# Looking up 4-bit weights: maxima of four neighbouring lines in one VectorE reduction

## The chip, the cores and the metric

The kernel runs on one core of one Trainium2 chip. The metric is the device time of one execution in microseconds (us), the median of the runs given. Lower is better.

## The reference

A decoder layer: self-attention, cross-attention, and a gated feed-forward stage whose three weight matrices are stored as 4-bit codes with one scale for each 64 codes. The change concerns the last stage alone:

```
NF4_CODE = [-1.0, -0.696, -0.525, -0.395, -0.284, -0.185, -0.091, 0.0,
            0.080, 0.161, 0.246, 0.338, 0.441, 0.563, 0.723, 1.0]
def dequant_nf4(q, absmax, shape):
    w = NF4_CODE[q.reshape(-1)]
    w = w.reshape(-1, 64) * absmax[:, None]
    return w.reshape(shape)
g = einsum('bsh,mh->bsm', x, Wg);  u = einsum('bsh,mh->bsm', x, Wu)
h = silu(g) * u
return einsum('bsm,hm->bsh', h, Wd)      # B*S = 2048, H = 1024, M = 3584
x = x + ffn(layernorm(x), ...)
```

## The kernel before

The program has two parts, one after the other: `attention` (up to about 930 us of the profiled execution) and `feed_forward`. Every engine runs its own list of instructions in the order of the code; semaphores are the only ties between them.

**The feed-forward stage.** The 3584 hidden features are worked in 14 groups of two chunks of 128. For each group the TensorE multiplies the normalised input with the gate and up weights (`gate_up`, L1507: 8 steps `q`, each one chunk against 512 columns, 24 matmuls for gate and 24 for up) and then adds the group's share of the output (`down`, L1527: 16 row blocks `r`, 12 matmuls each). Every product is three fp16 matmuls (high by high, high by low, low by high). Group 0 is written out, because the layer norm and the transposes of the input run within its first steps; groups 1 to 12 are a hardware loop; group 13 is written out again.

**A weight tile** is 128x512 codes. There are 12 a group, and they are worked six tiles ahead of their use. A tile goes through these steps:

1. SyncE loads codes and scales (`load`).
2. ScalarE draws eight lines (`draw_line`, L1553 and L1556): an affine function of the code each, an fp32 plane of 128x512. The code table, taken as a function of the code, is the maximum of four upper lines less the maximum of four lower lines. The first of each four is clamped at zero (`Relu`), the others are `Copy` with scale and bias.
3. VectorE takes three maxima on each side, pair by pair (L1631), and the difference of the two (L1637) into `w32`: seven operations, `LUT = 7` (`look_up`).
4. GpSimd multiplies by the scales (L1432), ScalarE casts to fp16 (`cut_high`, L1561), GpSimd computes the rest that fp16 lost (`cut_low`, L1437).

There is one set of eight planes, `line`. ScalarE draws one tile ahead of VectorE, so line `m` of the next tile may be drawn once VectorE has read line `m` of this one: that is the wait on `lut` in `draw_line`.

**The order around it.** `CUTS` (and `FIRST_CUTS` in group 0) says how many look-up operations VectorE has done by each step `q`. In groups 1 to 12 ten tiles lie in the eight gate and up steps and two in `down`, one operation behind each `add_down` (L1672). Each step's list on VectorE ends with `hidden(q)` (L1667), which needs the `silu` of that step from ScalarE (`gate_silu`, L1584) and the up product. ScalarE's lists follow the same cuts one tile later: `silu` stands three quarters through the lines of its step, `hidden_high` (L1589) behind the second line, `cut_high` behind the third line of a tile. TensorE has two banks each for gate, up and down: gate step `q` needs `silu(q - 2)`, down block `r` needs `add_down(r - 2)`, and `add_down(0)` stands behind `hidden(7)` on VectorE.

Of the kernel before, what the change touches and what calls it, by code (L numbers as in the profile page):

```python
# [8 lines left out]
FP32 = mybir.dt.float32  # L9
# [3 lines left out]
ALU = mybir.AluOpType  # L13
ACT = mybir.ActivationFunctionType
AX_X = mybir.AxisListType.X
# [6 lines left out]
P = 128  # L22
# [8 lines left out]
HALF = 512  # L31
# [17 lines left out]
def code_line(lo, hi):  # L49

    slope = np.float32(F_SCALE * (NF4[hi] - NF4[lo]) / (hi - lo))
    return float(slope), float(np.float32(F_SCALE * NF4[lo] - float(slope) * lo))
# [4 lines left out]
UPPER_LINES = [code_line(8, 9), code_line(10, 11), code_line(12, 13), code_line(14, 15)]  # L57
LOWER_LINES = [tuple(-v for v in code_line(*at)) for at in ((5, 6), (3, 4), (1, 2), (0, 1))]


LINES = [line for pair in zip(UPPER_LINES, LOWER_LINES) for line in pair]
NL = len(LINES)
LUT = 7


class Attention:
# [1193 lines left out]
def feed_forward(nc, dram):  # L1260

    with ExitStack() as ctx:
        def sb(name, shape, dt):
            return ctx.enter_context(nc.sbuf_tensor(name, shape, dt))
# [15 lines left out]
        dn_l = sb("dn_l", [P, 2, C], FP16)  # L1280
        codes = sb("codes", [P, 2, HALF], INT32)
        scales = sb("scales", [P, 2, HALF], FP32)
        line = sb("line", [P, NL, HALF], FP32)
        above = sb("above", [P, 1], FP32)
        below = sb("below", [P, 1], FP32)
        w32 = sb("w32", [P, 2, HALF], FP32)
# [16 lines left out]
        consts = sem("consts")  # L1303
# [8 lines left out]
        lined = sem("lined")  # L1312
        lut = sem("lut")
        scaled = sem("scaled")
        w_high = sem("fw_high")
        w_low = sem("fw_low")
# [14 lines left out]
        NQ = 2 * NB  # L1331
        AHEAD = 6
# [11 lines left out]
            return (2, (k - 6) // 2, k % 2) if k < 10 else (3, 0, k % 2)  # L1344


        CUTS = [0, 9, 18, 27, 36, 45, 54, 62, 70, 84]
        FIRST_CUTS = [-14, -7, 0, 7, 14, 28, 42, 56, 70, 84]

        def cuts_of(first):  # L1350
            return FIRST_CUTS if first else CUTS


        def ended_in(q, first):
            lo, hi = cuts_of(first)[q:q + 2]
            return range(lo // LUT, hi // LUT)

        def lines_in(q, first):
            lo, hi = cuts_of(first)[q:q + 2]
            return range(NL + lo * NL // LUT, NL + hi * NL // LUT)  # L1360

# [3 lines left out]
        def last_k(last):  # L1365
            return 6 if last else PER
# [46 lines left out]
        @block.gpsimd  # L1413
        def _(pool):
            nc.gpsimd.memset(ident[:, :], 0.0).then_inc(consts, 1)
            nc.gpsimd.memset(minus_half[:, :], -0.5).then_inc(consts, 1)
            nc.gpsimd.memset(zero[:, :], 0.0).then_inc(consts, 1)
            nc.gpsimd.memset(above[:, :], LINES[0][1]).then_inc(consts, 1)
            nc.gpsimd.memset(below[:, :], LINES[1][1]).then_inc(consts, 1)
            pool.wait_ge(consts, 5)  # L1420
            nc.gpsimd.affine_select(out=ident[:, :], in_=ident[:, :], compare_op=ALU.not_equal, fill=1.0, base=0,
                                    pattern=[[-1, P]], channel_multiplier=1).then_inc(consts, 1)

            def held(ge_sem, value):
                pool.wait_ge(ge_sem, value)
                pool.sem_inc(pool_tick, 1)

            def scale(i, k):
                t, w = AHEAD + PER * i + k, w32[:, k % 2, :]
                held(scales_loaded[k % 2], 32 * (PER // 2 * i + (AHEAD + k) // 2 + 1))  # L1430
                held(lut, LUT * (t + 1))
                nc.gpsimd.tensor_tensor(w, w, scales[:, k % 2, :], ALU.mult).then_inc(scaled, 1)  # L1432

            def cut_low(i, k):
                w_h, w_l = weights(*tile_of(k))
                held(w_high, AHEAD + PER * i + k + 1)
                nc.gpsimd.tensor_tensor(w_l, w32[:, k % 2, :], w_h, ALU.subtract).then_inc(w_low, 1)  # L1437

            def ln_root(r):
                s = slice(r % SLOTS, r % SLOTS + 1)  # L1440
                pool.wait_ge(ln_stat, 4 * r + 4)
                nc.gpsimd.tensor_tensor(rstd[:, s], var_eps[:, s], minus_half[:, :], ALU.pow).then_inc(ln_rstd, 1)
                nc.gpsimd.tensor_tensor(neg_mean[:, s], zero[:, :], mean_var[:, r % SLOTS, 0:1], ALU.subtract)\
                    .then_inc(ln_rstd, 1)
                pool.wait_ge(ln_rstd, 3 * r + 2)
                nc.gpsimd.tensor_tensor(shift[:, s], neg_mean[:, s], rstd[:, s], ALU.mult).then_inc(ln_rstd, 1)

            def hidden_low(i, q):
                cols = slice(T * (q % NB), T * (q % NB) + T)
                held(h_high, NQ * i + q + 1)  # L1450
                nc.gpsimd.tensor_tensor(hT_l[:, q // NB, cols], h32[:, q % 2, :], hT_h[:, q // NB, cols],  # L1451
                                        ALU.subtract).then_inc(h_low, 1)

            def group(i, last, first=False):
                for q in range(NQ + 1):
                    if q > 0:
                        hidden_low(i, q - 1)
                    for k in ended_in(q, first):
                        if k < last_k(last):
                            scale(i, k)  # L1460
                            if not rows_of_step(q, first):
                                cut_low(i, k)
                    for r in rows_of_step(q, first):
                        if r + LEAD < RT:
                            ln_root(r + LEAD)
                    if rows_of_step(q, first):
                        for k in ended_in(q, first):
                            cut_low(i, k)

            pool.sem_inc(h_low, FREE)  # L1470
            for k in range(-AHEAD, -2):
                scale(0, k)
                cut_low(0, k)
            for r in range(8 + LEAD):
                ln_root(r)
            group(0, False, True)
            with pool.Fori(1, GROUPS - 1) as i:
                group(i, False)
            group(GROUPS - 1, True)
# [63 lines left out]
        def _(act):  # L1543
            def draw_line(i, at):
                k, m = at // NL, at % NL
                t, slot = AHEAD + PER * i + k, k % 2
                if m == 0:
                    act.wait_ge(codes_loaded[slot], 16 * (PER // 2 * i + (AHEAD + k) // 2 + 1))
                if k > -AHEAD:
                    act.wait_ge(lut, LUT * (t - 1) + min(m + 1, LUT))  # L1550
                slope, intercept = LINES[m]
                if m < 2:
                    op = nc.scalar.activation(line[:, m, :], codes[:, slot, :], ACT.Relu, scale=slope,  # L1553
                                              bias=(above if m == 0 else below)[:, :])
                else:
                    op = nc.scalar.activation(line[:, m, :], codes[:, slot, :], ACT.Copy, scale=slope, bias=intercept)  # L1556
                op.then_inc(lined, 1)

            def cut_high(i, k):
# [62 lines left out]
        def _(dve):  # L1622
            def look_up(i, ops):
                for at in ops:
                    k, n = at // LUT, at % LUT
                    t = AHEAD + PER * i + k
                    if n < LUT - 1:
                        dve.wait_ge(lined, NL * t + n + 3)
                        if n >= 2:
                            dve.wait_ge(lut, LUT * t + n - 1)  # L1630
                        nc.vector.tensor_tensor(line[:, n + 2, :], line[:, n, :], line[:, n + 2, :], ALU.max)\  # L1631
                            .then_inc(lut, 1)
                    else:
                        dve.wait_ge(lut, LUT * t + n)
                        if k >= 2 - AHEAD:
                            dve.wait_ge(w_low, t - 1)
                        nc.vector.tensor_tensor(w32[:, k % 2, :], line[:, NL - 2, :], line[:, NL - 1, :], ALU.subtract)\  # L1637
                            .then_inc(lut, 1)

            def ln_stats(r):  # L1640
                s = r % SLOTS
# [34 lines left out]
            def group(i, last, first=False):  # L1676
                cuts = cuts_of(first)
                for q in range(NQ):
                    look_up(i, range(cuts[q], min(cuts[q + 1], LUT * last_k(last))))
                    hidden(i, q)  # L1680
                    ln_rows(rows_of_step(q, first))
                for r in range(RT):
                    add_down(i, r)
                    if cuts[NQ] + r < LUT * last_k(last) and r < cuts[NQ + 1] - cuts[NQ]:
                        look_up(i, range(cuts[NQ] + r, cuts[NQ] + r + 1))

            look_up(0, range(-LUT * AHEAD, -2 * LUT))
            for r in range(LEAD):
# [66 lines left out]
```

## Time and profile before

| what | value |
|---|---|
| time, median of 2 runs | 2774.8 us (2773.41 to 2776.2) |
| the profiled execution | 2782.7 us, of which the span of its trace is 2780.8 us |
| TensorE busy | 2577.7 us (93%) |
| VectorE busy | 2052.3 us (74%) |
| ScalarE busy | 1573.1 us (57%) |
| GpSimd busy | 1234.9 us (44%) |
| granted TensorE clock, mean | 0.968 |

The shares are averages over both parts. The feed-forward stage takes the span from about 934 us on. The profiled execution is 8 us longer than the median of the runs.

### The profile page before, as it was taken

The page shows a single profiled execution, that of the slowest core. Times are in us where ns is not written, and L with a number is a line of the kernel's source. Part 1 is how long each engine was busy: PE and PEld are TensorE (multiplying, and loading weights), DVE is VectorE, ACT ScalarE, POOL GpSimd, SP SyncE. Part 2 cuts the span into 40 slices and gives each one's busy share as a digit, 9 for nine tenths or more (in the row PEclk, how much of TensorE's full clock was granted, in tenths as well). Part 3 has the DMA queues.
Part 4 walks back from the last instruction along what each step waited for, and adds up shares of the span by engine and source line. Part 5 has one row for each costly group of instructions (what it writes and reads, how often), then busy time and mean ns, then how long its engine had stood idle before and what let it go on. Part 6 is the DMA issues. An engine that isn't in the chain of part 4 may idle for free.

```text
span 2780.8 us, 52667 instructions
## 1 busy us (share of the span) xinstructions
PE 2577.7 (93%) x18536; PEld 1395.6 (50%) x18536; DVE 2052.3 (74%) x2844; ACT 1573.1 (57%) x2794; POOL 1234.9 (44%) x1068
## 2 busy tenths in 40 slices
PE   5899999999965269899999999999999999999999
PEld 3567677776754134344444444444444444444444
DVE  6656678767666768778787869788787868778773
ACT  3566666656662477465564647465564747465550
POOL 2456677767783334243433425243343425243330
PEclk9999999999987679999999999999999999999999
DMA  5343343342312502121111111111111112111112
GB/s 193 94 151 96 108 135 114 98 130 76 96 51 67 183 23 64 46 62 39 53 53 46 61 38 60 46 60 40 59 53 39 60 42 66 37 60 49 50 34 121
DMA packets 153268, 205.34 MB, mean 74 GB/s; under 512 B 34160, under 2 KB 85872, under 8 KB 153072
## 3 DMA queue, kind: packets, MB, share of 16 engines
q1 hardware_dynamic: 153072, 202.97, 23.2%
q8 instruction: 93, 1.52, 0.2%
q14 instruction: 103, 0.84, 0.1%
HBM read 157.16 MB, written 44.04 MB: 72 GB/s over the span
## 4 chain that ended last, share of the span: by engine, by line
PE 61%; DVE 2%; issue 1%; ACT 1%; DMA 1%; POOL 0%; SPq 0%; DVEq 0%; ACTq 0%; POOLq 0%
PE f_bank L1507 40%; PE f_down L1527 21%; DVE line L1631 1%; DMA codes<-in_codes 1%; DVE f_stats L1645 0%; DVE fT_l L1658 0%; ACT line L1556 0%; ACT f_xn L1567 0%; PE f_down L1489 0%; ACT fT_h L1575 0%; DVE w L1637 0%; ACT line L1553 0%; DVE h L1667 0%; DVE y L1672 0%; DVE f_mean_var L1648 0%
## 5 line engine op out<-in xcount | busy, mean ns | idle before, releaser
L1631 DVE TENSOR_TENSOR line<-line 128x512 f32<-128x512 f32 x1008 | 920.9, 963 | 45.8 <-issue 29.8
L1556 ACT ACTIVATE line<-codes 128x512 f32<-128x512 int32 x1008 | 591.2, 620 | 383.6 <-DVE line L1631 285.6
L1507 PE MATMUL f_bank<-fT_h,up_h 128*128 128x512 f16 x1792 | 681.0, 380 | 3.7 <-DVE fT_l L1658 2.4
L1507 PE MATMUL f_bank<-fT_l,up_h 128*128 128x512 f16 x1792 | 680.9, 380 | 0.0
L1507 PE MATMUL f_bank<-fT_h,up_l 128*128 128x512 f16 x1792 | 680.7, 380 | 0.0
L538 POOL TENSOR_TENSOR p_l<-p,p_h 128x512 f16<-128x512 f32 x320 | 370.0, 1164 | 230.7 <-ACT p_h L951 230.1
L1672 DVE SCALAR_TENSOR_TENSOR y<-f_down,y 128x1024 f32<-128x1024 f32 x224 | 274.2, 1224 | 191.2 <-PE f_down L1527 191.2
L1437 POOL TENSOR_TENSOR up_l<-w,up_h 128x512 f16<-128x512 f32 x112 | 146.8, 1310 | 529.2 <-ACT up_h L1561 529.2
L1432 POOL TENSOR_TENSOR w<-w,scales 128x512 f32<-128x512 f32 x168 | 263.8, 1570 | 229.1 <-DVE w L1637 229.1
L1121 DVE TENSOR_REDUCE block_max<-bank 128x4 f32<-128x512 f32 x320 | 219.1, 687 | 185.3 <-PE bank L710 182.7
L1527 PE MATMUL f_down<-dn_h,hT_h 128*128 128x512 f16 x896 | 340.8, 380 | 9.0 <-DVE y L1672 9.0
L1527 PE MATMUL f_down<-dn_h,hT_l 128*128 128x512 f16 x896 | 340.6, 380 | 0.0
L1527 PE MATMUL f_down<-dn_l,hT_h 128*128 128x512 f16 x896 | 340.6, 380 | 0.0
L943 ACT ACTIVATE p<-bank 128x512 f32<-128x512 f32 x320 | 190.9, 597 | 260.1 <-PE bank L739 258.7
L1507 PEld LDWEIGHTS f_bank<-fT_h,up_h 128*128 128x128 f16 x1792 | 175.7, 98 | 214.9 <-DVE fT_l L1658 2.8
L1507 PEld LDWEIGHTS f_bank<-fT_h,up_l 128*128 128x128 f16 x1792 | 175.7, 98 | 212.6 <-issue 1.9
L1507 PEld LDWEIGHTS f_bank<-fT_l,up_h 128*128 128x128 f16 x1792 | 175.7, 98 | 210.7 <-issue 1.1
L1451 POOL TENSOR_TENSOR hT_l<-h,hT_h 128x512 f16<-128x512 f32 x112 | 173.0, 1545 | 237.6 <-ACT hT_h L1589 237.6
L1553 ACT ACTIVATE line<-codes,above 128x512 f32<-128x512 int32 x168 | 119.9, 714 | 216.1 <-DVE line L1631 178.6
L680 PE MATMUL bank<-xT,w_h 128*128 128x512 f16 x720 | 218.8, 386 | 2.1 <-POOL vx_h L608 2.1
L1667 DVE SCALAR_TENSOR_TENSOR h<-f_bank,h 128x512 f32<-128x512 f32 x112 | 77.1, 688 | 164.5 <-PE f_bank L1507 156.6
L951 ACT ACTIVATE p_h<-p 128x512 f16<-128x512 f32 x320 | 192.0, 621 | 0.0
(157 smaller groups left out, 4230.4 us busy)
## 6 DMA issues: line engine op xcount, KB each, us to landing
codes<-in_codes SPq DMA_DIRECT2D x168, 256.0 KB, 3.0
scales<-in_scales SPq DMA_DIRECT2D x336, 128.0 KB, 2.9
nat_parts<-nat SPq DMA_DIRECT2D x48, 256.0 KB, 2.0
q_rows<-nat_parts SPq DMA_DIRECT2D x96, 128.0 KB, 2.8
x_unit<-in_x SPq DMA_DIRECT2D x64, 128.0 KB, 2.8
x<-x_unit SPq DMA_DIRECT2D x64, 128.0 KB, 2.6
y<-x SPq DMA_DIRECT2D x4, 2048.0 KB, 12.1
out<-y SPq DMA_DIRECT2D x16, 512.0 KB, 2.6
```

The costliest lines, as they stand in the source:

```text
L538: nc.gpsimd.tensor_tensor(p_l[:, n % 2, k, :], p32[:, f % 3, :], p_h[:, n % 2, k, :], ALU.subtract).then_inc(p_low, 1)
L680: mm = nc.tensor.matmul(dst[:, :], w[:, c, cols], xT[:, :, half, c, :], start=(c == 0 and m == 0), stop=(c == CT - 1 and m == 2))
L943: nc.scalar.activation(p32[:, f % 3, :], bank[T_BANK + T_OF[f % CHUNKS]][:, :], ACT.Exp, scale=SELF_SCALE).then_inc(t_exp, 1)
L951: nc.scalar.activation(p_h[:, n % 2, k, :], p32[:, f % 3, :], ACT.Copy).then_inc(p_high, 1)
L1121: nc.vector.reduce_max(block_max[:, n % PAIRS, k, :], bank[S_BANK + S_OF[k]][:, :].rearrange("p (a n) -> p a n", n=P), AX_X)\
L1432: nc.gpsimd.tensor_tensor(w, w, scales[:, k % 2, :], ALU.mult).then_inc(scaled, 1)
L1451: nc.gpsimd.tensor_tensor(hT_l[:, q // NB, cols], h32[:, q % 2, :], hT_h[:, q // NB, cols], ALU.subtract).then_inc(h_low, 1)
L1507: mm = nc.tensor.matmul(bank[(GATE, UP)[kind] + n % 2][:, :], w[:, chunk, kind, P * c:P * c + P], x[:, c, cols], start=(m == 0), stop=(m = ...
L1527: mm = nc.tensor.matmul(down_bank[r % 2][:, half, :], h[:, m // 3, rows], w[:, m // 3, cols], start=(m == 0), stop=(m == 5))
L1556: op = nc.scalar.activation(line[:, m, :], codes[:, slot, :], ACT.Copy, scale=slope, bias=intercept)
L1631: nc.vector.tensor_tensor(line[:, n + 2, :], line[:, n, :], line[:, n + 2, :], ALU.max)\
L1672: nc.vector.scalar_tensor_tensor(y[:, r, :], down_bank[r % 2][:, :, :].rearrange("p a n -> p (a n)"), 1.0 / (H_SCALE * F_SCALE), y[:, r, : ...
```

## The change

The eight lines of a tile are written as two planes of four neighbours: element `n` of each four lies beside the others (`line[P, 2, 512, 4]`), so that each ScalarE operation now writes every fourth word, 16 bytes apart. VectorE then takes the maximum of each four neighbours by one reduction over 128x512x4 (into `w32` for the upper side, into a new buffer `side` for the lower side), and subtracts: three operations a tile, `LUT = 3`. ScalarE may draw the four lines of a side of the next tile once that side's reduction is done. `LINES` is sorted by side, so the second `Relu` line comes fifth instead of second. The cuts are counted anew in threes; in `down` the two tiles' six operations stand behind every second `add_down`.

```diff
-LINES = [line for pair in zip(UPPER_LINES, LOWER_LINES) for line in pair]
+LINES = UPPER_LINES + LOWER_LINES
-LUT = 7
+LUT = 3
-        line = sb("line", [P, NL, HALF], FP32)
+        line = sb("line", [P, 2, HALF, NL // 2], FP32)
+        side = sb("side", [P, HALF], FP32)
-        CUTS = [0, 9, 18, 27, 36, 45, 54, 62, 70, 84]
-        FIRST_CUTS = [-14, -7, 0, 7, 14, 28, 42, 56, 70, 84]
+        CUTS = [0, 4, 8, 12, 15, 19, 23, 27, 30, 36]
+        FIRST_CUTS = [-6, -3, 0, 3, 6, 12, 18, 24, 30, 36]
@@ draw_line (ScalarE)
-                if k > -AHEAD:
-                    act.wait_ge(lut, LUT * (t - 1) + min(m + 1, LUT))
+                which, n = 2 * m // NL, m % (NL // 2)
+                if k > -AHEAD and n == 0:
+                    act.wait_ge(lut, LUT * (t - 1) + which + 1)
                 slope, intercept = LINES[m]
-                if m < 2:
-                    op = nc.scalar.activation(line[:, m, :], codes[:, slot, :], ACT.Relu, scale=slope,
-                                              bias=(above if m == 0 else below)[:, :])
+                out = line[:, which, :, n]
+                if n == 0:
+                    op = nc.scalar.activation(out, codes[:, slot, :], ACT.Relu, scale=slope,
+                                              bias=(above, below)[which][:, :])
                 else:
-                    op = nc.scalar.activation(line[:, m, :], codes[:, slot, :], ACT.Copy, scale=slope, bias=intercept)
+                    op = nc.scalar.activation(out, codes[:, slot, :], ACT.Copy, scale=slope, bias=intercept)
@@ look_up (VectorE)
-                    if n < LUT - 1:
-                        dve.wait_ge(lined, NL * t + n + 3)
-                        if n >= 2:
-                            dve.wait_ge(lut, LUT * t + n - 1)
-                        nc.vector.tensor_tensor(line[:, n + 2, :], line[:, n, :], line[:, n + 2, :], ALU.max)\
+                    w = w32[:, k % 2, :]
+                    if n < 2:
+                        dve.wait_ge(lined, NL * t + NL // 2 * (n + 1))
+                        if k > -AHEAD:
+                            dve.wait_ge(lut, LUT * t)
+                        if n == 0 and k >= 2 - AHEAD:
+                            dve.wait_ge(w_low, t - 1)
+                        nc.vector.reduce_max((w, side[:, :])[n], line[:, n, :, :], AX_X)\
                             .then_inc(lut, 1)
                     else:
-                        dve.wait_ge(lut, LUT * t + n)
-                        if k >= 2 - AHEAD:
-                            dve.wait_ge(w_low, t - 1)
-                        nc.vector.tensor_tensor(w32[:, k % 2, :], line[:, NL - 2, :], line[:, NL - 1, :], ALU.subtract)\
-                            .then_inc(lut, 1)
+                        dve.wait_ge(lut, LUT * t + 2)
+                        nc.vector.tensor_tensor(w, w, side[:, :], ALU.subtract).then_inc(lut, 1)
@@ group (VectorE), the loop over down blocks
-                    if cuts[NQ] + r < LUT * last_k(last) and r < cuts[NQ + 1] - cuts[NQ]:
-                        look_up(i, range(cuts[NQ] + r, cuts[NQ] + r + 1))
+                    if r % 2 == 0 and r // 2 < cuts[NQ + 1] - cuts[NQ]:
+                        n = cuts[NQ] + r // 2
+                        look_up(i, range(n, min(n + 1, LUT * last_k(last))))
```

VectorE in group 0, the end of step 3 and step 4 (two tiles). Before:

```order
L1667 SCALAR_TENSOR_TENSOR h32<-f_bank3,h32 128x512
L1631 TENSOR_TENSOR line<-line 128x512 x6
L1637 TENSOR_TENSOR w32<-line 128x512
L1631 TENSOR_TENSOR line<-line 128x512 x6
L1637 TENSOR_TENSOR w32<-line 128x512
L1667 SCALAR_TENSOR_TENSOR h32<-f_bank2,h32 128x512
```

The same place in the changed kernel:

```order
L1670 SCALAR_TENSOR_TENSOR h32<-f_bank3,h32 128x512
L1637 TENSOR_REDUCE w32<-line 128x512
L1637 TENSOR_REDUCE side<-line 128x512
L1641 TENSOR_TENSOR w32<-w32,side 128x512
L1637 TENSOR_REDUCE w32<-line 128x512
L1637 TENSOR_REDUCE side<-line 128x512
L1641 TENSOR_TENSOR w32<-w32,side 128x512
L1670 SCALAR_TENSOR_TENSOR h32<-f_bank2,h32 128x512
```

Seven operations a tile have become three; the step keeps its two tiles and its `hidden`.

ScalarE in group 0, step 3: the eight lines of one tile with `hidden_high`, `cut_high` and `silu` between them. Before:

```order
L1553 ACTIVATE line<-codes,above 128x512
L1553 ACTIVATE line<-codes,below 128x512
L1589 ACTIVATE hT_h<-h32 128x512
L1556 ACTIVATE line<-codes 128x512
L1561 ACTIVATE up_h<-w32 128x512
L1556 ACTIVATE line<-codes 128x512 x4
L1584 ACTIVATE h32<-f_bank1 128x512
L1556 ACTIVATE line<-codes 128x512
```

In the changed kernel:

```order
L1556 ACTIVATE line<-codes,above 128x512
L1559 ACTIVATE line<-codes 128x512
L1592 ACTIVATE hT_h<-h32 128x512
L1559 ACTIVATE line<-codes 128x512
L1564 ACTIVATE up_h<-w32 128x512
L1559 ACTIVATE line<-codes 128x512
L1556 ACTIVATE line<-codes,below 128x512
L1559 ACTIVATE line<-codes 128x512 x2
L1587 ACTIVATE h32<-f_bank1 128x512
L1559 ACTIVATE line<-codes 128x512
```

The number of lines ahead of `silu` is the same, seven; the second clamped line has moved to fifth place.

VectorE at the start of `down` in group 0. Before:

```order
L1672 SCALAR_TENSOR_TENSOR y<-f_down0,y 128x1024
L1631 TENSOR_TENSOR line<-line 128x512
L1672 SCALAR_TENSOR_TENSOR y<-f_down1,y 128x1024
L1631 TENSOR_TENSOR line<-line 128x512
L1672 SCALAR_TENSOR_TENSOR y<-f_down0,y 128x1024
```

In the changed kernel:

```order
L1675 SCALAR_TENSOR_TENSOR y<-f_down0,y 128x1024
L1637 TENSOR_REDUCE w32<-line 128x512
L1675 SCALAR_TENSOR_TENSOR y<-f_down1,y 128x1024
L1675 SCALAR_TENSOR_TENSOR y<-f_down0,y 128x1024
L1637 TENSOR_REDUCE side<-line 128x512
```

One operation behind every `add_down` has become one longer operation behind every second.

## Rows read from the trace of the kernel before

**Rows 1.** Busy time and count of each engine in two stretches, then granted clock, DMA.
```profile
1100.00:1200.00 100.00, 90.97 (x410) 40.47 (x408) 82.90 (x91) 55.72 (x97) 36.21 (x25) 0.95 0.16 49
1243.30:1367.70 124.40, 124.40 (x578) 56.41 (x577) 99.05 (x109) 70.85 (x124) 46.65 (x32) 1.00 0.16 52
```

**Rows 2.** What TensorE waited for from 1000 us on: us, times, longest.
```profile
PE f_down L1527 <- DVE y L1672: 9.0, 1, 9.0
```

**Rows 3.** The chain that ended last, group 1: start, us, what.
```profile
1160.31 82.88 PE f_bank L1507 x384
```

**Rows 4.** VectorE's groups: operation, shapes, count | busy us, mean ns | idle before.
```profile
L1631 DVE TENSOR_TENSOR line<-line 128x512 f32<-128x512 f32 x1008 | 920.9, 963 | 45.8 <-issue 29.8 <-ACT line L1556 11.2 <-ACT line L1553 4.8
L1637 DVE TENSOR_TENSOR w<-line 128x512 f32<-128x512 f32 x168 | 131.5, 783 | 5.1
L1156 DVE TENSOR_REDUCE s_top<-s 128x8 f32<-128x512 f32 x48 | 32.9, 686 | 1.7
```

**Rows 5.** VectorE's small reductions of the attention part, same columns.
```profile
L1131 DVE TENSOR_REDUCE row_max<-block_max 128x4 f32<-128x16 f32 x32 | 5.1, 161 | 0.1
L1134 DVE TENSOR_REDUCE row_max<-block_max 128x4 f32<-128x8 f32 x32 | 4.9, 152 | 0.0
L1133 DVE TENSOR_REDUCE row_max<-block_max 128x4 f32<-128x4 f32 x32 | 4.8, 150 | 0.0
```

**Rows 6.** ScalarE's groups, same columns.
```profile
L1556 ACT ACTIVATE line<-codes 128x512 f32<-128x512 int32 x1008 | 591.2, 620 | 383.6 <-DVE line L1631 285.6 <-DVE w L1637 93.6
L1553 ACT ACTIVATE line<-codes,above 128x512 f32<-128x512 int32 x168 | 119.9, 714 | 216.1 <-DVE line L1631 178.6 <-DMA codes<-in_codes 37.6
L1561 ACT ACTIVATE up_h<-w 128x512 f16<-128x512 f32 x112 | 69.2, 617 | 33.7 <-POOL w L1432 33.7
L1584 ACT ACTIVATE h<-f_bank 128x512 f32<-128x512 f32 x112 | 64.6, 577 | 14.5 <-PE f_bank L1507 14.5
L879 ACT ACTIVATE w_h<-x_unit 128x1024 f16<-128x1024 f32 x8 | 8.2, 1045 | 2.1 <-DMA x_unit<-in_w 2.0
```

**Rows 7.** ScalarE's timeline: six lines back to back. Start, us, what.
```profile
951.01 3.21 ACT L1556 ACTIVATE line<-codes 128x512 f32<-128x512 int32 x6
```

**Rows 8.** GpSimd's memsets; the first two write single elements far apart.
```profile
L602 POOL MEMSET v_parts<- 128x32 f16 x1 | 0.2, 236 | 0.0
L608 POOL MEMSET vx_h<- 64x8 f16 x2 | 0.3, 130 | 0.1
L1418 POOL MEMSET above<- 128x1 f32 x1 | 0.1, 113 | 0.0
```

**Rows 9.** VectorE's timeline in group 0, and at the end of group 1.
```profile
1049.75 3.69 DVE L1631 TENSOR_TENSOR line<-line 128x512 f32<-128x512 f32 x6
...
1064.12 0.69 DVE L1667 SCALAR_TENSOR_TENSOR h<-f_bank,h 128x512 f32<-128x512 f32 x1 [2.31 <-PE f_bank L1507]
...
1069.37 6.69 DVE L1631 TENSOR_TENSOR line<-line 128x512 f32<-128x512 f32 x6
...
1119.90 1.21 DVE L1672 SCALAR_TENSOR_TENSOR y<-f_down,y 128x1024 f32<-128x1024 f32 x1
...
1284.66 1.23 DVE L1672 SCALAR_TENSOR_TENSOR y<-f_down,y 128x1024 f32<-128x1024 f32 x1 [1.37 <-PE f_down L1527]
1288.50 1.90 DVE L1631 TENSOR_TENSOR line<-line 128x512 f32<-128x512 f32 x3 [2.61 <-issue]
```

**Rows 10.** TensorE's timeline after its wait in group 0.
```profile
1121.17 0.61 PE L1527 MATMUL f_down<-dn_h,hT_h 128*128 128x512 f16 x1 [9.03 <-DVE y L1672]
1121.57 0.63 PE L1527 MATMUL f_down<-dn_l,hT_h 128*128 128x512 f16 x1
...
1126.69 0.38 PE L1527 MATMUL f_down<-dn_l,hT_h 128*128 128x512 f16 x1
```

**Rows 11.** The chain that ended last, at the start of the feed-forward stage.
```profile
955.53 18.84 DMA codes<-in_codes
974.40 1.33 ACT line L1553 x2
```

More of the change, by code:

```diff
@@ L1418, in _ @@
             nc.gpsimd.memset(above[:, :], LINES[0][1]).then_inc(consts, 1)
-            nc.gpsimd.memset(below[:, :], LINES[1][1]).then_inc(consts, 1)
+            nc.gpsimd.memset(below[:, :], LINES[NL // 2][1]).then_inc(consts, 1)
             pool.wait_ge(consts, 5)
```

## The prediction

> **What bounds the kernel now.** I read the busy time of stretches first, then what TensorE waits for, then the groups and timelines of VectorE and ScalarE. From group 1 on TensorE is never idle: in a whole group, 124.4 us, it is busy for 124.40 [rows 1]. The gate and up half of a group takes it 82.9 us for 384 matmuls, 0.216 us each [rows 3], so a down block of 12 takes 2.59 us. From 1000 us on TensorE's only long wait is one of 9.0 us in group 0, for `add_down(0)`, which VectorE reaches at 1119.90 because it is behind [rows 2, 9]. In a steady group VectorE is busy for 99 us and ScalarE for 71 of 124 [rows 1]. Time that the change frees on VectorE can only be worth what group 0 loses: 9.0 us and the half clock behind it (0.50 granted, matmuls 0.427 us apart from 1121.17 to 1126.69, which costs 2.7 us against 13 at 0.216) [rows 10]. So the gain is capped at some 12 us, 0.4%. What matters is whether an engine that had room comes to need more than the slot that TensorE leaves it.
>
> **VectorE, part by part.** Removed per tile: six maxima. They take 3.69 us alone and up to 6.69 us when GpSimd works beside them [rows 9], 0.963 us each in the mean; the difference takes 0.783 [rows 4]. That is 6.6 us a tile. Added: two reductions of 2048 elements. Reductions of 512 take 0.686 us [rows 4] and of 16 take 0.161 [rows 5], so 1.06 ns an element, and 0.686 + 1536 x 0.00106 = 2.31 us each. With the difference a tile takes 5.3 us. Bounds: never under 2.2 us (the same slope without the fixed part), and 4.5 us if reading 2048 neighbours cost twice the slope, which no row suggests. Against GpSimd's contention a gain of about 1.3 us a tile; with no contention a loss of 0.9 us. In `down`, a pair of blocks holds 2 x 1.21 + 2.31 = 4.7 us of VectorE in TensorE's 5.18 us, so it still fits.
>
> **ScalarE, the part that decides.** Eight lines a tile stay eight, but each now writes words 16 bytes apart. Today a line takes 0.620 us, a clamped one 0.714 [rows 6], and back to back they follow each other at 0.52 us (six in 3.21) [rows 7]. ScalarE's slope is 0.83 ns an element (1024 in 1.045 us, 512 in 0.617) [rows 6]. No row shows ScalarE writing with a step. Call the spacing of lines a = 0.52 + 0.512e us, where e is what the step costs in ns an element. Nearest rows:
> - VectorE's small reductions write with a step of 16 bytes throughout; the smallest also reads its four elements as single words, 16 or 80 bytes apart. From 16 and 8 elements (161 and 152 ns) one expects 147.5 ns for 4, and it took 150 [rows 5]: 0.6 ns an element, a = 0.83. It is the same step and type, but four elements and mostly reading.
> - GpSimd's memset of 8 single elements takes 130 ns against 113 for one [rows 8]: 2.4 ns each, 1.6 over ScalarE's 0.83, a = 1.34. The one of 32 takes 236 ns, 4.0 each, 3.1 over, a = 2.1. These write, but with larger steps on a slower engine.
> - The lower end is e = 0, a = 0.52.
>
> I take one more of ScalarE's element times, e = 0.83, a = 0.945: an engine that passes one element per 0.83 ns should lose whole steps of that, and it lies between the two nearest rows, 0.6 and 1.6.
>
> The Trainium skill, "SBUF — State Buffer" (the box on cachelines under "Door 1: The DMA port swizzle"), says that full bandwidth needs at least two hits on each 16-byte line; four-word steps hit each line once. "Vector Engine (DVE) Microarchitecture Reference", section 5.2, gives VectorE 1.71 ns a column for a destination hopping 4 KiB each element and 2.50 for one stepping 24 words, against 1.05 contiguous. Estimates from that page, if ScalarE's port lost as much: a = 0.86 and 1.26, and some 2840 and 3300 us. No row here shows either on ScalarE; they speak against this change.
>
> **The sum for a steady group.** Let D be the end of the `down` before. VectorE's first look-up starts 3.85 us later (1288.50 against 1284.65; 2.61 of it are idle with nothing waited for, at the loop's branch) [rows 9]. Before, ScalarE could draw after the first short maximum; now it must wait for the whole first reduction: D + 6.15. Up to the end of `silu(7)` it has 79 lines, 20 of them clamped (0.1 more each, 2.0), 10 `cut_high` and 7 `hidden_high` at 0.52 (8.8) and 8 `silu` at 0.48 (3.8): D + 20.8 + 79a. With `hidden(7)`, `add_down(0)` and 0.1 us of signals, `y` is ready at D + 22.8 + 79a. TensorE wants it after 82.9 + 2 x 2.59, at D + 88.1. So TensorE stands still for **79a - 65.3 us**, and the turning point is a = 0.827. Below it the wait of ScalarE for VectorE (today 383.6 us of idle time ahead of the `Copy` lines alone [rows 6]) takes up the extra work, and nothing is lost. With a = 0.945: 9.4 us, and after a pause like the one in [rows 10] the clock is at half for 2.7 us more: 12.1 a group. Groups 1 to 12 have it, 145 us; group 13 has only six tiles, and none. In `down` ScalarE has two tiles in 41.5 us, so each group starts without debt.
>
> **Group 0.** Steps 0 and 1: `silu` comes 1.6 us later (a reduction of 2.31 instead of a maximum of 0.69) and 7 x 0.425 for the lines, and the transposes of the next rows queue behind it on ScalarE, with TensorE behind them: 4.6 each, 9. Steps 2 and 3 took 15.1 us (1049.75 to 1064.81, with 2.3 us of waiting for TensorE) [rows 9]; now each needs reduction, seven lines, two casts, `silu` and `hidden`, 2.4 + 6.7 + 1.0 + 0.5 + 0.8 = 11.4: 8 more. Steps 4 to 7 took 13.8 each; sixteen lines and four other operations make 17.6: 15 more. Start: the loads of `y` are queued on SyncE behind the scales of an early tile, which wait for two tiles to be scaled: 6 us later; behind those loads come the codes that ScalarE waits for at 974.40 [rows 11], and eight lines follow: 3.4. Sum 41. TensorE's old 9.0 us lie inside this path and are not counted again.
>
> **Forecast:** 145 + 41 = 186 us. On the profiled execution that is 2782.7 + 186 = 2969; it was 8 us above the median of the runs, so **2961 us**, 6.7% slower.
>
> **Rivals.**
> - *The step costs ScalarE nothing* (not slower). Then a steady group is TensorE's alone. Group 0: 3 us later in steps 0 and 1, 2 in steps 2 and 3, and in 4 to 7 the two engines hand the halves to each other in about 12.4 us a step instead of 13.8, 6 us gained: 2774 us. For it: nothing in the profile shows ScalarE slowed by anything. Against: rows 5 and 8. Chance 0.15. If all of group 0's wait went too, 2763; 2% faster is out of reach.
> - *A small cost, as in rows 5*: a = 0.83, right at the turning point. Some 4 us in the loop, and in group 0 with the start 8 + 6 + 8 + 5: 2805 us. Chance 0.13.
> - *One element time more*: 2961, between 2880 and 3060 for a from 0.88 to 1.03. Chance 0.42.
> - *Two or more, as the memset of 8*: a = 1.34. (40.6 + 2.7) x 12 = 520, group 0 and start about 85: 3380 us; the stretch up to it from 3060 belongs here. Chance 0.23. As the memset of 32, about 4200: 0.03.
> - *The reductions take 4.5 us*: VectorE needs 9.8 us a tile, ten tiles and eight `hidden` 103 us, some 21 us over, with the clock 24 x 12: about 3090 us. Chance 0.04.
>
> **Chances and range.** Slower by over 2% (above 2830): 0.42 + 0.23 + 0.03 + 0.04 = 0.72. Within 2%, about what a measurement of this kernel can tell from no change: 0.27. Faster: 0.01. The range runs from 2800, with the small cost inside, to 3420, above the memset's case; it leaves out the free step and the 32-element memset, 0.18.
>
> **What would show it.** The mean of a line on ScalarE: 1.05 us here, 0.62 for the free step, 0.93 at the turning point, 1.44 for the memset of 8. A reduction: 2.3 us. TensorE's wait at `f_down` for `y`: once in each of groups 1 to 12, about 9 us, each with a dip of the clock; with no slow lines, none but in group 0. GpSimd's multiplications should get shorter, since a one-input reduction stands beside them. I am wrong if the lines keep 0.62 us, or if they lengthen and TensorE still does not wait, which would mean that the order of the lists has more slack than I counted.

## The result, and the profile after

The changed kernel takes 2966.55 us (median of 2 runs, 2964.7 to 2968.4) against 2774.8 us: 1.069 times the time before, with a 95% interval of 1.0645 to 1.0737. The profiled execution took 2964.7 us with a span of 2962.9, 182.1 us more than the span before.

The groups of the page after, ScalarE's lines first (columns as in [rows 4]):

```profile
L1559 ACT ACTIVATE line<-codes 128x512 f32<-128x512 int32 x1008 | 1074.8, 1149 | 0.0
L1556 ACT ACTIVATE line<-codes,above 128x512 f32<-128x512 int32 x168 | 205.9, 1225 | 387.8 <-DVE w L1637 367.3
L1637 DVE TENSOR_REDUCE w<-line 128x512 f32<-128x2048 f32 x168 | 383.2, 2281 | 115.0 <-POOL dn_l L1438 51.0
L1637 DVE TENSOR_REDUCE side<-line 128x512 f32<-128x2048 f32 x168 | 382.9, 2279 | 92.8 <-ACT line L1559 92.7
L1433 POOL TENSOR_TENSOR w<-w,scales 128x512 f32<-128x512 f32 x168 | 214.2, 1275 | 120.0 <-DVE w L1641 120.0
```

Against [rows 6] a line has gone from 0.620 to 1.149 us and a clamped one from 0.714 to 1.225, with the same number of elements. ScalarE has less idle time left: ahead of the first clamped line and the `Copy` lines together it was 599.7 us [rows 6] and is 387.8. (The 0.0 ahead of the `Copy` lines only says that none of them waits now by itself; the first line of a side waits for all four.) VectorE has less to do than before (1886 us busy against 2052), and GpSimd's multiplication has become shorter, 1.275 us.

What TensorE waited for (us, times, longest), and one whole group between two `add_down(0)`, for all engines as in [rows 1]:

```profile
PE f_down L1528 <- DVE y L1675: 130.7, 13, 19.3
...
PE f_bank L1508 <- ACT h L1587: 5.1, 12, 0.5
```

```profile
1293.30:1429.44 136.14, 126.48 (x576) 56.60 (x576) 86.33 (x62) 107.37 (x125) 37.93 (x32) 0.96 0.15 47
```

Before, TensorE waited once at `f_down` [rows 2]; now once in each of 13 groups: 19.3 us in group 0 and 9.3 in each of the 12 of the loop. The group of the loop shown takes 136.1 us instead of the 124.3 between the same two instructions before, and holds the same matmuls; later groups take up to 136.6. The end of such a group's gate and up half, on VectorE, ScalarE and TensorE:

```profile
1428.17 0.63 ACT L1587 ACTIVATE h<-f_bank 128x512 f32<-128x512 f32 x1
```

```profile
1428.83 0.69 DVE L1670 SCALAR_TENSOR_TENSOR h<-f_bank,h 128x512 f32<-128x512 f32 x1 [5.34 <-ACT h L1587]
1429.44 1.22 DVE L1675 SCALAR_TENSOR_TENSOR y<-f_down,y 128x1024 f32<-128x1024 f32 x1
...
1430.71 0.61 PE L1528 MATMUL f_down<-dn_h,hT_h 128*128 128x512 f16 x1 [9.28 <-DVE y L1675]
1431.11 0.63 PE L1528 MATMUL f_down<-dn_l,hT_h 128*128 128x512 f16 x1
...
1434.89 0.38 PE L1528 MATMUL f_down<-dn_l,hT_h 128*128 128x512 f16 x1
```

Read backwards: TensorE waited 9.28 us for `add_down(0)`, which stood behind `hidden(7)`, which had waited 5.34 us for `silu(7)` on ScalarE, and that stood behind ScalarE's lines. After the wait the matmuls are 0.427 us apart up to 1434.89 instead of 0.216, which costs 2.0 us more. 9.3 + 2.0 and 0.4 for the wait on `silu` in the middle of a group make 11.7 of the 12 us or so by which a group is longer.

The 182 us: `add_down(0)` of group 0 starts at 1157.32 instead of 1119.90 [rows 9], 37.4 us later. That of group 12, first line below, starts at 2794.43; before, second line, it was 2613.33:

```profile
2794.43 1.21 DVE L1675 SCALAR_TENSOR_TENSOR y<-f_down,y 128x1024 f32<-128x1024 f32 x1
```

```profile
2613.33 1.23 DVE L1672 SCALAR_TENSOR_TENSOR y<-f_down,y 128x1024 f32<-128x1024 f32 x1 [1.83 <-PE f_down L1527]
```

So the twelve stretches between them take 1637.1 us instead of 1493.4, 143.7 more, or 12.0 a group. The stretch behind takes 1.1 us more, with group 12's half clock in it, and the end is as long as before. 37.4 + 143.7 + 1.1 is all of the 182.

### The profile page after: what moved, and what is told of

Same layout as the page of the kernel before. It is cut to its first block, busy times and chain, and to the rows that moved or that the text cites. A ratio compares the mean times of both kernels' runs of the same rounds, so it can differ in the third digit from the quotient of the medians.

```text
span 2962.9 us, 50339 instructions
## 1 busy us (share of the span) xinstructions
PE 2610.4 (88%) x18536; PEld 1401.0 (47%) x18536; DVE 1886.2 (64%) x2172; ACT 2085.3 (70%) x2794; POOL 1113.4 (38%) x1068
## 4 chain that ended last, share of the span: by engine, by line
ACT 32%; PE 22%; DVE 6%; issue 5%; DMA 2%; POOL 1%; DVEq 0%; SPq 0%; ACTq 0%; POOLq 0%
ACT line L1559 20%; PE f_down L1528 18%; ACT line L1556 7%; DVE w L1637 4%; PE f_bank L1508 3%; DMA codes<-in_codes 2%; ACT h L1587 1%; ACT up_h L1564 1%; ACT hT_h L1592 1%; ACT dn_h L1564 1%; DVE y L1675 1%; POOL w L1433 0%; DVE f_stats L1648 0%; DVE fT_l L1661 0%; POOL hT_l L1452 0%
## 5 line engine op out<-in xcount | busy, mean ns | idle before, releaser
L1559 ACT ACTIVATE line<-codes 128x512 f32<-128x512 int32 x1008 | 1074.8, 1149 | 0.0
L1556 ACT ACTIVATE line<-codes,above 128x512 f32<-128x512 int32 x168 | 205.9, 1225 | 387.8 <-DVE w L1637 367.3
L1528 PE MATMUL f_down<-dn_h,hT_h 128*128 128x512 f16 x896 | 351.7, 393 | 130.7 <-DVE y L1675 130.7
L1637 DVE TENSOR_REDUCE w<-line 128x512 f32<-128x2048 f32 x168 | 383.2, 2281 | 115.0 <-POOL dn_l L1438 51.0
L1438 POOL TENSOR_TENSOR up_l<-w,up_h 128x512 f16<-128x512 f32 x112 | 129.9, 1160 | 846.5 <-ACT up_h L1564 846.5
L1637 DVE TENSOR_REDUCE side<-line 128x512 f32<-128x2048 f32 x168 | 382.9, 2279 | 92.8 <-ACT line L1559 92.7
L1528 PE MATMUL f_down<-dn_l,hT_h 128*128 128x512 f16 x896 | 350.0, 391 | 0.0
L1528 PE MATMUL f_down<-dn_h,hT_l 128*128 128x512 f16 x896 | 349.2, 390 | 0.0
L1433 POOL TENSOR_TENSOR w<-w,scales 128x512 f32<-128x512 f32 x168 | 214.2, 1275 | 120.0 <-DVE w L1641 120.0
L1556 ACT ACTIVATE line<-codes,below 128x512 f32<-128x512 int32 x168 | 203.7, 1213 | 21.7 <-DVE side L1637 21.7
## 6 DMA issues: line engine op xcount, KB each, us to landing
y<-x SPq DMA_DIRECT2D x4, 2048.0 KB, 12.4
```

What stands on the lines that cost most here:

```text
L1528: mm = nc.tensor.matmul(down_bank[r % 2][:, half, :], h[:, m // 3, rows], w[:, m // 3, cols], start=(m == 0), stop=(m == 5))
L1556: op = nc.scalar.activation(out, codes[:, slot, :], ACT.Relu, scale=slope, bias=(above, below)[which][:, :])
L1559: op = nc.scalar.activation(out, codes[:, slot, :], ACT.Copy, scale=slope, bias=intercept)
L1637: nc.vector.reduce_max((w, side[:, :])[n], line[:, n, :, :], AX_X)\
```

## The experiments

The theory (A): writing single words 16 bytes apart slows ScalarE's lines, and past a turning point its list up to `silu(7)` makes TensorE wait. The rivals: the reductions or the hand-over by four lines cost the time (B); each slow line costs its share, with no turning point (C). Ratios are against the kernel before on the same chip, which took 2779.7 us beside write_contig, write_step2, read_step and late_redraw3, and 2780.0 us beside half_step, later_cuts, swap_targets and pairs_cuts. The other two ran once, beside one run of it of 2781.5 us. The diffs are cut to what matters.

**write_contig: the step of the writes undone, all else kept.**

```diff
-                out = line[:, which, :, n]
+                out = line[:, which, P * n:P * n + P, :].rearrange("p a b -> p (a b)")
```

> The changed kernel with one thing undone: each line is written as 512 neighbouring words again, into the same region that the reduction of its side reads; waits, order, cuts and reductions stay. The reduction then takes the maximum of other words than it should, which leaves out the look-up's meaning, not its work. Theory A (the step of ScalarE's writes is the whole loss): lines back to 0.62 us, reductions 2.28, groups of 124.4 us without a wait of TensorE, 2765 to 2785 us. Rival B (the reductions, or the hand-over of four lines at a time, cost the time): the lines get short and the total stays above 2900.

2782.0 us, ratio 1.0011 (0.9998 to 1.0024).

```profile
L1559 ACT ACTIVATE line<-codes 128x512 f32<-128x512 int32 x1008 | 583.9, 614 | 0.0
L1556 ACT ACTIVATE line<-codes,above 128x512 f32<-128x512 int32 x168 | 121.3, 722 | 699.6 <-DVE w L1637 673.9
L1637 DVE TENSOR_REDUCE w<-line 128x512 f32<-128x2048 f32 x168 | 383.2, 2281 | 50.0 <-ACT line L1559 26.0
```

The reductions take as long as in the changed kernel, and the semaphore waits in the program are the same; only the lines are short again, 0.614 us, and no loss clear of noise is left. That is theory A, and B is out.

**write_step2: a step of two words.**

```diff
-                out = line[:, which, :, n]
+                out = line[:, which, 256 * (n // 2):256 * (n // 2) + 256, :] \
+                    .rearrange("p a (c d) -> p (a c) d", d=2)[:, :, n % 2]
```

> The same with a step of two words (8 bytes) instead of four, again into the same region and with the reductions as they are (their maxima are over other words). If it is a question of how many words of 16 neighbouring bytes are hit (two here): 0.62 us a line and 2765 to 2785 us. If any step costs ScalarE the same: 1.15 us a line and 2950 to 2980. If the cost grows with the step: 0.8 to 0.9 us, no wait in the loop, 2790 to 2810.

2784.1 us, ratio 1.0006 (0.9995 to 1.0017).

```profile
L1559 ACT ACTIVATE line<-codes 128x512 f32<-128x512 int32 x1008 | 625.0, 661 | 0.0
```

A line takes 0.661 us, 0.05 more than with neighbouring words, and 0.49 less than with a step of four. A step as such is nearly free.

**write_step8: a step of eight words.**

```diff
-                out = line[:, which, :, n]
+                out = line[:, which, :, :].rearrange("p (r two) n -> p r (two n)", two=2)[:, :, 2 * n:2 * n + 2] \
+                    .rearrange("p r c -> p c r")      # the codes are read as "p (c r) -> p c r", c=2
```

> The changed kernel with a step of eight words (32 bytes) in two passes of 256, into the same region (the maxima are over other words). If the cost is one per single word whatever the step: 1.15 us a line, 2955 to 2975 us. If it grows with the step: 1.3 us or more a line and above 3050 us.

One run: 2969.9 us.

```profile
L1559 ACT ACTIVATE line<-codes 128x512 f32<-128x512 int32 x1008 | 1070.3, 1142 | 0.0
```

1.142 us, as with a step of four. So the cost does not grow from four words to eight; the edge lies between two and four. The Trainium skill, "SBUF — State Buffer" (the box on cachelines), asks for two hits on each 16-byte line: a step of two words hits each line twice, and steps of four and eight once, and on this rule the three durations agree. "Vector Engine (DVE) Microarchitecture Reference", section 5.2, gives a higher cost for one small step (24 words) than for large ones; no run here tried that step, and at four and eight words ScalarE shows no such difference.

**read_step: the planes kept, the step moved into VectorE's read.**

```diff
-        line = sb("line", [P, 2, HALF, NL // 2], FP32)
+        line = sb("line", [P, 2, NL // 2, HALF], FP32)
-                out = line[:, which, :, n]
+                out = line[:, which, n, :]
-                        nc.vector.reduce_max((w, side[:, :])[n], line[:, n, :, :], AX_X)
+                        nc.vector.reduce_max((w, side[:, :])[n], line[:, n, :, :].rearrange("p n h -> p h n"), AX_X)
```

> The reductions are kept but the planes too: ScalarE writes 512 neighbouring words, VectorE's reduction reads its four elements 2048 bytes apart and goes on by one word. Theory A: lines 0.62 us. If VectorE's reads with a step are free: reductions 2.28 us, 2765 to 2785 us. If they cost what ScalarE's writes cost (0.75 ns an element): 3.8 us each, 8.4 a tile, ten tiles and the eight hidden products 90 us against a slot of 87, so a wait of TensorE of some 3 to 5 us in each of 12 groups, 2830 to 2870 us.

2970.5 us, ratio 1.0683 (1.0665 to 1.0701), worse than any of the figures given.

```profile
L1637 DVE TENSOR_REDUCE w<-line 128x512 f32<-128x2048 f32 x168 | 639.0, 3804 | 12.4 <-ACT line L1559 9.1
...
L1559 ACT ACTIVATE line<-codes 128x512 f32<-128x512 int32 x1008 | 585.3, 616 | 0.0
```

```profile
PE f_down L1528 <- DVE y L1675: 143.2, 59, 21.9
```

The lines are short and the reduction takes 3.80 us instead of 2.28: (3804 - 2281) / 2048 = 0.74 ns more an element, just the price expected. The price was right and what hangs on it was counted too small. Ahead of `add_down(0)` TensorE waits 7.5 us in each group of the loop and not 3 to 5: VectorE, which has no room left there, also waits for `silu` four times, 4.6 us in the group from 1285 to 1422, which the sum of its busy times leaves out. Another 2.6 us a group are lost in `down` (TensorE waits 59 times at `f_down` in all), where two additions of 1.21 and one reduction of 3.8 us make 6.2 us, and two blocks take TensorE 5.2. That the total equals the changed kernel's is chance; another engine sets it.

**late_redraw3: the kernel before with a coarser hand-over.**

```diff
-                    act.wait_ge(lut, LUT * (t - 1) + min(m + 1, LUT))
+                    act.wait_ge(lut, LUT * (t - 1) + min(m + 3, LUT))
```

> The kernel before with the hand-over alone made coarser: line m of the next tile waits for operation m + 3 instead of m + 1, about 2 us later, as the reduction does. Theory A: it has room in the loop, where ScalarE idles 384 us ahead of its lines; only group 0 gets later, 2775 to 2790 us. Rival B (the coarser hand-over is a main part): above 2830.

2786.4 us, ratio 1.0025 (1.001 to 1.0039). A later hand-over costs some 7 us. In the profiled execution `add_down(0)` of group 0 starts 3.9 us later and the groups of the loop are as long as before, as A says.

**half_step: only the lower side is written with the step.**

```diff
-                out = line[:, which, :, n]
+                out = line[:, which, :, n] if which else line[:, 0, P * n:P * n + P, :].rearrange("p a b -> p (a b)")
```

> The changed kernel with the step undone on the upper side only (its maxima are then over other words); the lower side still writes every fourth word. Turning point as forecast (TensorE waits 79a - 65.3 us a group, a the mean spacing of lines): a is about 0.73, under 0.827, so no wait in the loop, only group 0 and the start are later: 2785 to 2805 us. Rival C (each slow line costs its share, no turning point): half of the loss, 2865 to 2880.

2798.1 us, ratio 1.0067 (1.0051 to 1.0082).

```profile
L1559 ACT ACTIVATE line<-codes 128x512 f32<-128x512 int32 x1008 | 821.5, 881 | 0.0
```

```profile
PE f_down L1528 <- DVE y L1675: 8.9, 1, 8.9
```

ScalarE has half of the extra work, and TensorE waits at `f_down` once, in group 0, not in the loop. A tenth of the loss is left, not half: there is a turning point, and it lies above a mean spacing of 0.72 us, which is what the `Copy` lines have in the loop here. C is out. The formula counts too much room below it, though: `silu(7)` ends 3.7 us before it would make TensorE wait, where 65.3 - 79a gives 8.4, since ScalarE also waits for first reductions, 5.8 us a group here. Where between 0.72 and the 0.93 us of the changed kernel the point lies was not tried.

**later_cuts: two look-up operations moved behind the gate and up half.**

```diff
-        CUTS = [0, 4, 8, 12, 15, 19, 23, 27, 30, 36]
+        CUTS = [0, 4, 7, 11, 14, 18, 21, 25, 28, 36]
```

> The changed kernel with other cuts in groups 1 to 12: 28 instead of 30 look-up operations ahead of down, 8 in it, and 6 lines fewer ahead of silu(7) on ScalarE. If ScalarE's list up to silu(7) sets the wait, it shrinks by 6 x 0.94 = 5.6 us a group and the half clock gets shorter: 2880 to 2900 us. If the loss comes from ScalarE's sum over the group or from VectorE, nothing changes: 2960 to 2970.

2870.4 us, ratio 1.0328 (1.0313 to 1.0343); 96 us less than the changed kernel with the same slow lines (1.151 us each).

```profile
PE f_down L1528 <- DVE y L1675: 54.3, 17, 19.4
```

```profile
1286.40 0.39 PE L1528 MATMUL f_down<-dn_h,hT_h 128*128 128x512 f16 x1 [2.74 <-DVE y L1675]
...
1287.16 0.63 PE L1528 MATMUL f_down<-dn_h,hT_h 128*128 128x512 f16 x1
...
1290.47 0.38 PE L1528 MATMUL f_down<-dn_h,hT_l 128*128 128x512 f16 x1
...
1544.17 0.39 PE L1528 MATMUL f_down<-dn_h,hT_h 128*128 128x512 f16 x1 [2.66 <-DVE y L1675]
```

Outside group 0 34.9 us of waiting are left, 2.9 a group instead of 9.3. So the place of the six lines ahead of `silu(7)` counts, not ScalarE's sum over the group. The gain in the loop is 7.8 us a group, above the 5.6 that were expected beside some half clock: 6.4 of the wait at `f_down`, 0.4 of the one on `silu`, which is gone, and 0.8 of half clock. The half clock itself mostly stays: behind a wait of 2.7 us it still costs 1.7 us in eight of the twelve groups (matmuls of 0.63 us above, from 1287.16), and nothing in the other four (1544.17 begins `down` behind the wait in one of these).

**swap_targets: VectorE's wait for GpSimd moved behind the first reduction.**

```diff
-                        if n == 0 and k >= 2 - AHEAD:
+                        if n == 1 and k >= 2 - AHEAD:
                             dve.wait_ge(w_low, t - 1)
-                        nc.vector.reduce_max((w, side[:, :])[n], line[:, n, :, :], AX_X)\
+                        nc.vector.reduce_max((side[:, :], w)[n], line[:, n, :, :], AX_X)\
-                        nc.vector.tensor_tensor(w, w, side[:, :], ALU.subtract).then_inc(lut, 1)
+                        nc.vector.tensor_tensor(w, side[:, :], w, ALU.subtract).then_inc(lut, 1)
```

> The changed kernel with the targets of the two reductions exchanged (upper side into side, lower side into w32), so that VectorE waits for GpSimd's cut_low of two tiles ago before the second reduction and not before the first. That wait ahead of the first reduction was not in the forecast; ScalarE stands 2.9 us a group behind it. If it costs on the path: 12 x up to 2.9 and some 1 us a step in group 0, 2925 to 2950 us. If it is covered: 2960 to 2970.

2962.3 us, ratio 1.0663 (1.0645 to 1.068), beside 1.0691 (1.0645 to 1.0737) of the changed kernel, measured in other runs.

```profile
ACT line L1556 <- DVE side L1637: 367.1, 82, 14.1
```

VectorE's wait for GpSimd is gone, and ScalarE's for VectorE is the same as in the changed kernel, 367.1 against 367.3 us. The loop's groups are as long; `add_down(0)` of group 0 starts 2.0 us earlier, at 1155.30. The wait is covered in the loop.

**seven_ops_step4: the layout of the change with the seven operations of before.** Line `m` lies at `line[:, m % 2, :, m // 2]`, for ScalarE and VectorE alike; nothing else differs from the kernel before.

```diff
-        line = sb("line", [P, NL, HALF], FP32)
+        line = sb("line", [P, 2, HALF, NL // 2], FP32)
-                        nc.vector.tensor_tensor(line[:, n + 2, :], line[:, n, :], line[:, n + 2, :], ALU.max)\
+                        nc.vector.tensor_tensor(line[:, n % 2, :, n // 2 + 1], line[:, n % 2, :, n // 2],
+                                                line[:, n % 2, :, n // 2 + 1], ALU.max)\
```

> The kernel before with the layout of the change alone: planes interleaved by four, the seven two-input operations and the fine hand-over kept. ScalarE's lines at 1.15 us again set the time: at least the loss of the changed kernel, 2950 to 3050 us, more if VectorE's operations, which now read two streams and write one with a step, take 1.06 us or more each (7.4 a tile and above, with GpSimd beside it 9). Rival B (reductions are part of the loss): under 2900.

One run: 3177.4 us.

```profile
L1556 ACT ACTIVATE line<-codes 128x512 f32<-128x512 int32 x1008 | 1064.8, 1145 | 207.8 <-DVE line L1631 156.3
L1631 DVE TENSOR_TENSOR line<-line 128x512 f32<-128x512 f32 x1008 | 1143.5, 1200 | 38.7 <-issue 25.5
```

The lines are as slow as in the changed kernel without any reduction, and the maxima, which read and write with the step too, go from 0.963 to 1.200 us. The time is above 3050 us, as was expected for maxima of over 1.06 us: besides 170.6 us at `f_down`, TensorE waits 120.8 us for `silu` within the gate and up steps, where the changed kernel has 5.1. With this layout the reduction is the better reader: its words are neighbours.

**pairs_cuts: the reductions without single words.** Lines lie in pairs (`line[P, 2, 2, HALF, 2]`), ScalarE writes with a step of 8 bytes, and the reduction reads two neighbours, hops 4096 bytes and reads two more. Its targets are exchanged as in swap_targets (not shown below), and in group 0 two look-up operations have moved into `down`.

```diff
-                out = line[:, which, :, n]
+                out = line[:, which, n // 2, :, n % 2]
-                        nc.vector.reduce_max((w, side[:, :])[n], line[:, n, :, :], AX_X)\
+                        nc.vector.reduce_max((side[:, :], w)[n], line[:, n, :, :, :].rearrange("p a h d -> p h a d"),
+                                             mybir.AxisListType.XY)\
-        FIRST_CUTS = [-6, -3, 0, 3, 6, 12, 18, 24, 30, 36]
+        FIRST_CUTS = [-6, -3, 0, 3, 6, 11, 17, 22, 28, 36]
```

> A version that keeps the two reductions and computes the same as the reference: lines lie in pairs, ScalarE writes with a step of 8 bytes, the reduction reads two neighbours, hops 4096 bytes and reads two more; targets exchanged as in swap_targets; and in group 0 two look-up operations moved from steps 4 to 7 into down. If runs of two words are read at the full rate: lines 0.66 us, reductions 2.28, no wait in the loop, and the wait in group 0 (9.0 us before) gone or nearly: 2763 to 2774 us. If the hops cost as single words do (0.74 ns an element on half of them): reductions 3.0 us, still under the slot, 2770 to 2785.

2779.0 us, ratio 0.9994 (0.9982 to 1.0006).

```profile
L1559 ACT ACTIVATE line<-codes 128x512 f32<-128x512 int32 x1008 | 624.5, 660 | 0.0
...
L1637 DVE TENSOR_REDUCE side<-line 128x512 f32<-128x2048 f32 x168 | 383.3, 2281 | 24.7 <-ACT line L1559 22.0
```

Runs of two words are read at the full rate (2.281 us) and written nearly so. Of TensorE's waits the one at `f_down` is gone altogether; in the profiled execution the span is 2775.9 us against 2780.8. The gain falls short of the 2763 to 2774 us that were expected for these durations: `add_down(0)` of group 0 starts only 3.3 us earlier (1116.62), since the first steps are later (`hidden(3)` by 3.9 us), and what is left cannot be told from no change. The change as an idea can be had without its loss; there is nothing for it to win while TensorE is busy for the whole loop.

## Why the prediction was right

2961 us were forecast and 2966.55 measured, on the likeliest case of those named.

- *The turning point and the wait.* TensorE's wait of 79a - 65.3 us a group: the `Copy` lines of the loop follow each other at 0.93 us in the mean, which gives 8.2 us, and the trace has 9.3. half_step lies below the point and has no wait, later_cuts takes six lines out of the count and has 2.9 us. That ScalarE's list up to `silu(7)` sets the wait, and that there is a turning point, is shown; the formula's 0.827 for it was not tried, and counts too much room below it (half_step). The half clock behind the wait costs 2.1 us a group in the mean, not 2.7.
- *The price of the step.* One more element time of ScalarE, 0.83 ns, was a choice between 0.6 and 1.6. Measured in the loop 0.80 (0.93 us), and 0.74 at the start of the stage, where three lines take 2.70 us. That the choice came so near is in part luck: the reason given, that whole element times are lost, is shown by no run, and both figures are under one. The mean duration forecast with it, 1.05 us, was too small (1.149): a slow line overlaps the next by some 0.2 us, not 0.1, and it is the spacing that counts.
- *Two errors that nearly cancel, by luck.* VectorE's first look-up was put 3.85 us behind D, with 2.61 us of idle time at the loop's branch. In the changed kernel it follows `add_down(15)` after 1.14 us, so ScalarE starts 2.7 us earlier than forecast. Against that ScalarE waits 3.9 us a group for a first reduction, which was not in the sum: that reduction stands behind `hidden`, which waits for `silu`. Together they add 1.2 us, which with the 8.2 above makes 9.4. Why the idle time went was not tried.

```profile
1372.55 1.23 ACT L1556 ACTIVATE line<-codes,above 128x512 f32<-128x512 int32 x1 [0.98 <-DVE w L1637]
...
1383.83 1.24 ACT L1556 ACTIVATE line<-codes,above 128x512 f32<-128x512 int32 x1 [1.92 <-DVE w L1637]
...
1420.60 1.22 ACT L1556 ACTIVATE line<-codes,above 128x512 f32<-128x512 int32 x1 [0.99 <-DVE w L1637]
```

- *VectorE.* A reduction was put at 2.31 us and takes 2.28. With short lines it costs nothing, as write_contig shows; with slow ones ScalarE meets it three times a group, in the 3.9 us above.
- *A wait not counted.* The first reduction writes `w32` at once and so waits for GpSimd's `cut_low` of two tiles ago, where before only the last of seven operations did. It adds up to 99 us on VectorE and is covered in the loop (swap_targets). Where it shows is the rival of the free step: write_contig needs 13.55 us for a step of two tiles in group 0, not the 12.4 of the forecast, with 1.44 us of this wait in each:

```profile
1110.44 0.69 DVE L1670 SCALAR_TENSOR_TENSOR h<-f_bank,h 128x512 f32<-128x512 f32 x1 [1.10 <-ACT h L1587]
...
1117.69 2.29 DVE L1637 TENSOR_REDUCE w<-line 128x512 f32<-128x2048 f32 x1 [1.44 <-POOL up_l L1438]
...
1123.99 0.69 DVE L1670 SCALAR_TENSOR_TENSOR h<-f_bank,h 128x512 f32<-128x512 f32 x1 [1.10 <-ACT h L1587]
```

- *Group 0 and the start*: 41 us forecast, 37.4 measured. By the times of `hidden`, steps 0 and 1 are 9.1 us later (9 forecast), 2 and 3 7.7 (8), 4 to 7 14.7 (15). The difference lies in the start, 6.0 us instead of 9.4: the codes that were awaited at 974.40 come at 977.41, 3 us later and not 6.
- *Sum*: 145 and 41 forecast; 144 and 37 measured, and 1 behind.

## What to carry to other kernels

Before operations are merged on one engine, ask who has to write or read in a new pattern for it: the operand's step was the dear part here, on an engine that the change did not mean to touch. Room on an engine is to be counted up to the instruction that someone waits for, not over the whole loop: ScalarE was busy for 107 of 136 us and still set the time, and moving six lines behind that instruction gave half of the loss back. A wait goes into such a count as well as the busy times: the 3.9 us here and the 4.6 us of read_step were in no sum. Where neighbours were wanted, pairs of fp32 words were enough here.

## What the runs showed of the hardware

- ScalarE, 512 fp32 words written: 0.614 us as neighbours, 0.661 with a step of 8 bytes, 1.149 with 16, 1.142 with 32.
- VectorE, a reduction of 2048 fp32 words to 512: 2.28 us when the four lie side by side, 2.28 when they lie in two pairs 4096 bytes apart, 3.80 when each lies 2048 bytes from the next.
- Six two-input maxima of 512 fp32 words, back to back, took 3.69 us alone and 6.69 beside GpSimd's operations [rows 9]; one took 0.963 in the mean of the whole stage [rows 4]. The one-input reduction kept its 2.28 us whether GpSimd worked beside it or not, and GpSimd's multiplication went from 1.570 us in the mean to 1.275.
- A wait of TensorE of 9.3 us was followed by 4.2 us at half clock, the one of 9.0 us before by 5.5 us [rows 10], and one of 2.7 us by some 3.5 us at half clock in eight groups of later_cuts and by none in four.
